# A two-layer decoder in one launch: another order of jobs in its relative attention, and weights of the last FFN rounded inside the expert stage

## What is computed

```python
# sublayer 3: routed FFN, 64 experts of 256 -> 1024 -> 256, the best 3 per token
logits = xf @ gate_w + gate_b
top_l, top_i = jax.lax.top_k(logits, 3)
...
# sublayer 5: attention on the context with relative distances clipped to +-32, 16 heads of 16
attn = softmax((rq @ rk.T + rq . rel_k_table[idx]) / 4)
w1 = attn @ rv
w2 = einsum("bhqk,qkd->bhqd", attn, rel_v_table[idx])
x = (w1 + w2).reshape(b, t, 256) @ Wo + bo
# sublayer 6: FFN with weights rounded to 4 bits in blocks of 32 and activations to 16 bits
s = max(abs(wb).max(-1) / 7, 1e-12); wq = round(wb / s) * s
up = act_qdq(x @ wq_up.T); gate = act_qdq(x @ wq_gate.T)
o = act_qdq(act_qdq(gate * sig) * up); return o @ wq_down.T
```

## Time and profile before

| what | value |
|---|---|
| median of 3 runs | 2712.79 us (2708.49 to 2713.68) |
| the profiled execution | 2708.04 us |
| its span on the core | 2706.3 us |
| mean granted TensorE clock | 0.928 |
| PE busy | 2334.3 us, 86% |
| DVE busy | 1496.6 us, 55% |
| ACT busy | 1247.3 us, 46% |
| POOL busy | 628.4 us, 23% |
| moved by DMA | 339.40 MB, 125 GB/s over the span |

### The profile page before, as it was taken

How to read it: one execution, slowest core, us unless ns; L and a number is a source line. 1 busy time by engine, 2 the same in 40 slices (tenths; PEclk the granted TensorE clock), 3 DMA queues, 4 the chain that set the end, 5 groups by cost and what they waited for, 6 DMA issues and landing times. The chain is left out here.

```text
span 2706.3 us, 52950 instructions
## 1 busy us (share of the span) xinstructions
PE 2334.3 (86%) x18240; PEld 1856.8 (69%) x18240; DVE 1496.6 (55%) x2887; ACT 1247.3 (46%) x2737; POOL 628.4 (23%) x690
## 2 busy tenths in 40 slices
PE   8989999967999999669979999999999996695047
PEld 5669999867999999558855666666666664452035
DVE  5866666675111111158865666666566664644865
ACT  2223333211334334248855565556555554436753
POOL 1101111156434444544441111211111110000000
PEclk9999999958999999879989999999999997797579
DMA  2122223172999999620025554555555452110111
GB/s 82 46 80 67 66 74 74 27 266 72 339 340 343 345 343 346 194 68 0 0 35 142 123 128 119 127 125 124 128 123 126 119 126 57 46 55 0 53 45 43
DMA packets 375990, 339.40 MB, mean 125 GB/s; under 512 B 70226, under 2 KB 351852, under 8 KB 374636
## 3 DMA queue, kind: packets, MB, share of 16 engines
q1 hardware_dynamic: 311148, 294.82, 36.6%
q10 hardware_dynamic: 52480, 26.83, 3.9%
q0 software_dynamic: 12288, 16.79, 2.8%
HBM read 255.03 MB, written 83.37 MB: 125 GB/s over the span
## 5 line engine op out<-in xcount | busy, mean ns | idle before, releaser
L2212 ACT COPY rel_probT<-rel_ps_t 121x400 f32<-121x400 f32 x384 | 196.3, 511 | 255.4 <-PE rel_ps_t L2424 255.4
L2224 ACT ACTIVATE rel_prob<-rel_ps_s,rel_nmx 100x361 f32<-100x361 f32 x512 | 264.8, 580 | 1.3 <-DVE rel_nmx L2301 1.2
L2424 PEld LDWEIGHTS rel_ps_t<-rel_ident,rel_prob 100*121 100x121 f32 x1536 | 196.4, 186 | 77.9 <-ACT rel_probT L2212 49.2
L2424 PE MATMUL rel_ps_t<-rel_ident,rel_prob 100*121 100x100 f32 x1536 | 243.1, 281 | 7.2 <-ACT rel_probT L2212 7.2
L1328 PEld LDWEIGHTS moe_ps_h<-moe_xeT,moe_w 128*128 128x128 f32 x2048 | 240.2, 193 | 5.1 <-issue 1.9
L1328 PE MATMUL moe_ps_h<-moe_xeT,moe_w 128*128 128x128 f32 x2048 | 240.8, 276 | 1.3 <-DVE moe_xeT L1493 1.3
L2301 DVE TENSOR_REDUCE rel_nmx<-rel_ps_s 100x2 f32<-100x722 f32 x256 | 232.8, 909 | 8.8
L1328 PE MATMUL moe_ps_y<-moe_w,moe_hT 128*128 128x256 f32 x1024 | 231.4, 379 | 0.0
L2944 PE MATMUL ffd_ps_y<-ffn_w_dT,ffd_oq 128*100 128x256 f32 x384 | 85.8, 385 | 139.8 <-DVE ffd_oq L2889 134.2
L1319 ACT ACTIVATE moe_hT<-moe_ps_h,moe_b 128x128 f32<-128x128 f32 x512 | 142.8, 376 | 137.5 <-PE moe_ps_h L1328 137.1
L1328 PEld LDWEIGHTS moe_ps_y<-moe_w,moe_hT 128*128 128x128 f32 x1024 | 189.6, 190 | 23.2
(11 more groups left out here) (430 smaller groups left out, 4975.9 us busy)
## 6 DMA issues: line engine op xcount, KB each, us to landing
moe_w<-in_L_ffn_w SPq DMA_DIRECT2D x128, 1024.0 KB
rel_scores<-rel_r_ext SPq DMA_DIRECT2D x32, 818.8 KB
rel_r_key<-rel_scores SPq DMA_DIRECT2D x32, 818.8 KB
rel_weights<-rel_prob ACTq DMA_DIRECT2D x128, 204.7 KB
rel_by_dist<-rel_weights SPq DMA_DIRECT2D x32, 400.0 KB
mut_ctx_nat<-in_ctx SPq DMA_DIRECT2D x32, 363.0 KB
mut_ctx_T<-in_ctxT SPq DMA_DIRECT2D x16, 722.0 KB
rel_ctx_T<-in_ctxT SPq DMA_DIRECT2D x32, 361.0 KB
```

The lines of the kernel that those rows point to most:

```text
L2212: nc.scalar.copy(probT[:, pg % 2, c], ps_pT).then_inc(s_t_sb, 1)
L2224: last = nc.scalar.activation(prob[:, t.parity, slot, :], ps_s[0:S, j, 0:L], ACT.Exp, bias=nmx[:, slot:slot + 1])
L2424: last = nc.tensor.transpose(ps_pT[:, j, :], prob[:, pt.parity, QUAD * pg + j, c * STEP:c * STEP + R], ident[0:S, 0:S])
```

## The change

**In relative attention** `JOBS` and `PLACES` get another order. `den` moves from the third quad to the second, ahead of `r1`; `v2` moves from the fourth quad to the third; `d0` is now alone at the end of the third quad, after `v2`, and `d1` early in the fourth; `w2` and `out` come one place later. VectorE copies `rel_raw` between the two pairs of maxima of the second quad, and sums the far distances after the maxima of the third quad instead of after the takes of the second. A new semaphore, `s_half`, counts the first two exponentials of a quad: TensorE waits for it before the first scores, and for `s_p` only before the third.

**The rounding of the FFN weights** goes into a class `QuantisedAhead`. Its three loads stand in SP's queue of the routed FFN, behind those for causal attention. Its 18 steps are issued by VectorE, one after each of the experts 42 to 59; these rounds are written out instead of looped. The buffers `hot01`, `bv` and one of zeros are left out, with others used in their place, and the transfers of zeros for relative attention are waited for by SP in the block of causal attention, no longer in that of relative attention.

**In the preparation block** VectorE norms the first 12 batches itself, ScalarE the other 20; the maxima of all eight groups follow; the transposes of the down matrix get three PSUM banks of their own, copied by VectorE between maxima. The buffer `up_kept` is allocated after this block.

```diff
--- before.py
+++ after.py
...
+class QuantisedAhead:
...
+    STEPS = 18
...
+    def load(self, sp):
...
+        sp.dma_start(self.w_in[:, 0], io["L1_ffn_w_up"].rearrange("(c p) d -> p c d", p=P)).then_inc(self.s_w[0], 16)
+        sp.dma_start(self.w_in[:, 1], io["L1_ffn_w_gate"].rearrange("(c p) d -> p c d", p=P)).then_inc(self.s_w[1], 16)
+        sp.dma_start(self.w_d[:], io["L1_ffn_w_down"].rearrange("(c p) d -> p c d", p=P)).then_inc(self.s_w[2], 16)
+
+    def step(self, dve, i):
+        nc, n, k = self.nc, i // 6, i % 6
+        blocks = self.flat[n].rearrange("p (b k) -> p b k", k=self.BLOCK)
+        if i > 0:
+            dve.wait_ge(self.s_q, i)
+        if k == 0:
+            dve.wait_ge(self.s_w[n], 16)
+            nc.vector.tensor_reduce(self.top[:], blocks, AX.X, ALU.max, apply_absolute_value=True).then_inc(self.s_q, 1)
+        elif k == 1:
+            nc.vector.tensor_scalar(self.step_[:], self.top[:], 1.0 / 7.0, TINY, ALU.mult, ALU.max).then_inc(self.s_q, 1)
+        elif k == 2:
+            nc.vector.reciprocal(self.inv[:], self.step_[:]).then_inc(self.s_q, 1)
+        elif k == 3:
+            nc.vector.tensor_tensor(blocks, blocks, self.inv[:].unsqueeze(2).to_broadcast([P, self.NB, self.BLOCK]),
+                                    ALU.mult).then_inc(self.s_q, 1)
+        elif k == 4:
+            nc.vector.tensor_scalar(blocks, blocks, ROUND, ROUND, ALU.add, ALU.subtract).then_inc(self.s_q, 1)
+        else:
+            nc.vector.tensor_tensor(blocks, blocks, self.step_[:].unsqueeze(2).to_broadcast([P, self.NB, self.BLOCK]),
+                                    ALU.mult).then_inc(self.s_q, 1)
...
             ahead.load(sp)
+            quantised.load(sp)
             sp.wait_ge(s_zero, 1)
...
+            def last_expert(t):
+                expert(t)
+                if isinstance(t.i, int) and STILL <= t.i < STILL + quantised.STEPS:
+                    quantised.step(dve, t.i - STILL)
+
+            STILL = E - 2 - DEEP * 5
+            rounds(dve, last_expert, -2, 2, STILL, E, DEEP)
...
-            sp.dma_start(self.p_rows[v, :, :, 0:self.REACH], self.zeros[:, :, 0:self.REACH]).then_inc(self.s_zero, 16)
+            sp.dma_start(self.r_rows[v, :, :, self.NEAR:self.RW], zeros[:]).then_inc(self.s_zero, 16)
+            sp.dma_start(self.p_rows[v, :, :, 0:self.REACH], zeros[:, :, 0:self.REACH]).then_inc(self.s_zero, 16)
+        sp.wait_ge(self.s_zero, 64)
...
         AHEAD = {"after": 2, "next": 1, "last": -1}
         JOBS = [("after", "xT"), ("next", "k0"), ("after", "q"), ("next", "k1"), ("after", "r0"), ("next", "v0"),
-                ("after", "r1"), ("next", "v1"), ("last", "den"), ("last", "d0"), ("last", "d1"), ("last", "w2"),
-                ("next", "v2"), ("last", "out")]
-        PLACES = [[0], [1], [2], [3], [4], [5], [6], [], [7], [8], [9, 10], [], [11], [12], [13], []]
+                ("last", "den"), ("after", "r1"), ("next", "v1"), ("next", "v2"), ("last", "d0"), ("last", "d1"),
+                ("last", "w2"), ("last", "out")]
+        PLACES = [[0], [1], [2], [3], [4], [5], [6], [7], [], [8], [9], [10], [], [11], [12], [13]]
...
-            sp.wait_ge(s_zero, 64)
...
-                if k == 1:
-                    last.then_inc(s_p, 1)
+                last.then_inc(s_p if k else s_half, 1)
...
                     maxima(t, g, 0)
-                    maxima(t, g, 1)
                     if g == 1 and prev.within(B):
                         dve.wait_ge(s_pv, GROUPS * prev.i + GROUPS)
                         nc.vector.tensor_copy(raw[:], ps_raw).then_inc(s_att, 1)
+                    maxima(t, g, 1)
+                    if g == 2 and prev.within(B):
+                        dve.wait_ge(s_far, prev.i + 1)
+                        dve.wait_ge(s_pdist, 16 * prev.i + 16)
+                        nc.vector.reduce_sum(by_dist[:, :, 0], far[:], AX.X).then_inc(s_far_sum, 1)
                     for k in range(4):
...
-                    if g == 1 and prev.within(B):
-                        dve.wait_ge(s_far, prev.i + 1)
-                        dve.wait_ge(s_pdist, 16 * prev.i + 16)
-                        nc.vector.reduce_sum(by_dist[:, :, 0], far[:], AX.X).then_inc(s_far_sum, 1)
...
-                pe.wait_ge(s_p, GROUPS * t.i + (g + 1))
+                pe.wait_ge(s_half, GROUPS * t.i + (g + 1))
...
+                    if j == 2:
+                        pe.wait_ge(s_p, GROUPS * t.i + (g + 1))
                     last = mm(ps_s[0:S, j, 0:L], q_par[rows, t.parity, g % 2, g // 2, :], kT[rows, t.parity, g // 2, :], 0, 1)
...
-                sp.dma_start(w_in[:, 0], io["L1_ffn_w_up"].rearrange("(c p) d -> p c d", p=P)).then_inc(s_w[0], 16)
...
+                def largest(g):
+                    nc.vector.tensor_reduce(row_top[:, g:g + 1], y_nat[:, g * G:(g + 1) * G, :], AX.XY, ALU.max,
+                                            apply_absolute_value=True).then_inc(s_top, 1)
+
+                for g in range(OWN):
+                    for b in range(g * G, (g + 1) * G):
+                        nc.vector.tensor_scalar(y_nat[:, b, :], y_nat[:, b, :], mean[:, b:b + 1], rstd[:, b:b + 1],
+                                                ALU.subtract, ALU.mult).then_inc(s_own, 1)
+                for g in range(OWN):
+                    dve.wait_ge(s_own, (g + 1) * G)
+                    largest(g)
+                for g in range(OWN, GROUPS):
+                    dve.wait_ge(s_x, (g - OWN + 1) * G)
+                    largest(g)
+                    if g - OWN < IC // 2:
+                        i = g - OWN
+                        dve.wait_ge(s_d, i + 1)
+                        nc.vector.tensor_copy(w_dT[:, 2 * i:2 * i + 2, :].rearrange("p e d -> p (e d)"),
+                                              ps_d[:, i, 0:2 * D]).then_inc(s_d_sb, 1)
+                dve.wait_ge(s_d_sb, IC // 2)
...
+                    if i == 3:
+                        for j, (parts, _) in enumerate(downs()):
+                            for e, tile in enumerate(parts):
+                                last = nc.tensor.transpose(ps_d[:, j, e * P:(e + 1) * P], tile, ident[:])
+                            last.then_inc(s_d, 1)
...
+                for b in range(OWN * G, B):
+                    nc.scalar.activation(y_nat[:, b, :], y_nat[:, b, :], ACT.Identity, bias=shift[:, b:b + 1],
+                                         scale=rstd[:, b:b + 1]).then_inc(s_x, 1)
...
```

## The result

The forecast was 2681. The profiled execution has a span of 2677.1 us at a mean granted clock of 0.933 (before: 2706.3, 0.928).

What follows compares the result with a forecast made beforehand. Relative attention was taken as bound by TensorE's program, routing and last-FFN preparation by DVE. Routing +6, preparation -19.2, expert steps 0, turns -19.6, last turn +0.3, semaphores/code +0.5 sum to -32.0 from 2712.79: 2681 us, range 2660 to 2702.

## What to carry to other kernels

When jobs are placed by hand between producer and consumer, write down for each pair the time from the producer to its consumer's release (here 1.31 us from one set of transposes to the next, and 5.96 from scores to the last exponential) and see that each has at least that much work between: the same jobs in another place were worth more than the finer semaphore. A step on the engine that feeds others, like the far sum, belongs into its idle time, even if an input arrives only just before. And a load that is needed late should stand in its queue behind the transfers that somebody waits for.

## What was not expected of the hardware

- A finer wait can make a wait invisible: of the 17.5 us, some 15 reappeared as busy time of the same group (89.2 to 105.2 us, of which one belongs to eight more products).
- The same program's last turns differ by 6.3 us between two executions, with 0.50 of the clock in different windows, while its steady turns repeat to 0.01 us (0.06 for the kernel before).
- The price of a job depends on its successor: the output product took 1.03 us ahead of scores and 0.95 ahead of transposes. The cause stays open.
